# Hybrid layers on one core: a four-tile top-k search with sums on TensorE, weight halves kept in DRAM for the scans, and the product with D moved behind the second group's scan

## The reference

```python
# state space layer: a scan over 512 tokens, 1024 channels, 16 states each
dA = jnp.exp(dt_t[..., None] * A)
state = state * dA + (dt_t * u_t)[..., None] * B_t[:, None, :]
y = jnp.einsum('bdn,bn->bd', state, C_t)
...
y = ys + x * D
y = y * silu(gate)

# top-k feed-forward: of 1376 values per row the 688 smallest in size become 0
s = silu(x @ w_gate.T)
_, idx = top_k(-abs(s), 688)
s = s.at[rows, idx].set(0) * (x @ w_up.T)
out = s @ w_down.T
```

## Time and profile before

| | us |
|---|---|
| median of 3 runs | 2920.8 (2917.94 to 2924.18) |
| the profiled execution | 2916.4, span 2914.6 |
| mean granted TensorE clock | 0.904 of full speed |
| first scan stage, about | 612 to 962 |
| second scan stage, about | 1098 to 1453 |
| search with its thresholds | 2560 to 2791 |

### The profile page before, as it was taken

How to read it: one execution, slowest core, us unless ns; L and a number is a source line. 1 busy time by engine, 2 the same in 40 slices (tenths; PEclk the granted TensorE clock), 3 DMA queues, 4 the chain that set the end, 5 groups by cost and what they waited for, 6 DMA issues and landing times.

```text
span 2914.6 us, 36546 instructions
## 1 busy us (share of the span) xinstructions
PE 2389.8 (82%) x12216; PEld 1868.3 (64%) x12216; DVE 2028.0 (70%) x3132; ACT 1596.3 (55%) x3341; POOL 1147.3 (39%) x986
## 2 busy tenths in 40 slices
PE   6986889858888866888889799998799998975058
PEld 4334337657777655777777578886678886764046
DVE  3642743659989657989853577875677875489896
ACT  1451551257787227887620276665176665499952
POOL 3022026343243514233357547674547674531100
PEclk9698799969999978999999899999999999985579
DMA  6214122120110111021023201121201121210000
GB/s 214 45 54 147 35 62 80 40 76 23 48 37 23 55 55 39 13 62 30 26 62 99 71 26 55 48 62 44 58 26 55 48 62 44 70 47 21 4 1 29
DMA packets 86257, 152.83 MB, mean 52 GB/s; under 512 B 8664, under 2 KB 17496, under 8 KB 85944
## 3 DMA queue, kind: packets, MB, share of 16 engines
q1 hardware_dynamic: 86072, 150.50, 18.1%
HBM read 135.33 MB, written 14.75 MB: 51 GB/s over the span
## 4 chain that ended last, share of the span: by engine, by line
PE 48%; DVE 18%; ACT 14%; issue 8%; POOL 1%; DVEq 0%; ACTq 0%; POOLq 0%
PE ps L659 42%; PE ps L673 5%; ACT tables L1402 5%; DVE m L1638 2%; DVE m L1664 2%; DVE f_lo L1464 2%; ACT m L1266 1%; DVE m_front L1585 1%; PE ps L798 1%; DVE loose L1567 1%; DVE f_hi L1463 1%; ACT L1266 1%; ACT m L1245 1%; DVE stat L1479 1%; ACT tables L1235 1%
## 5 line engine op out<-in xcount | busy, mean ns | idle before, releaser
L599 POOL TENSOR_SCALAR w_hi<-w_in 128x512 fp32r<-128x512 f32 x408 | 331.8, 813 | 1176.8 <-PE ps L659 614.7
L600 POOL TENSOR_TENSOR w_lo<-w_in,w_hi 128x512 fp32r<-128x512 f32 x408 | 607.6, 1489 | 34.0
L659 PE MATMUL ps<-hT_hi,w_lo 128*128 128x512 f32 x864 | 364.7, 422 | 28.5 <-DVE a L1509 12.3
L659 PE MATMUL ps<-hT_lo,w_hi 128*128 128x512 f32 x864 | 347.2, 402 | 0.0
L659 PE MATMUL ps<-hT_hi,w_hi 128*128 128x512 f32 x864 | 347.0, 402 | 0.0
L1664 DVE TENSOR_TENSOR_SCAN m<-m,m 128x1028 f32<-128x1028 f32 x128 | 315.9, 2468 | 10.3 <-ACT m L1266 3.1
L659 PEld LDWEIGHTS ps<-m,tables 128*128 128x128 f32 x2048 | 258.0, 199 | 53.6 <-ACT tables L1235 25.5
L659 PE MATMUL ps<-m,tables 128*128 128x128 f32 x2048 | 263.2, 284 | 33.0 <-ACT tables L1235 32.8
L673 PE MATMUL ps<-tables,m 128*128 128x128 f32 x1024 | 145.2, 285 | 99.4 <-DVE m L1664 71.4
L1235 ACT ACTIVATE tables<-ps 128x512 f32<-128x512 f32 x256 | 139.1, 593 | 147.2 <-PE ps L673 147.1
L1266 ACT ACTIVATE m<-m_rows,negA 128x256 f32<-128x256 f32 x512 | 217.8, 504 | 0.4
(11 more groups left out here) (256 smaller groups left out, 5269.1 us busy)
## 6 DMA issues: line engine op xcount, KB each, us to landing
w_in<-units SPq DMA_DIRECT2D x419, 256.0 KB, 2.6
stack_scratch<-a SPq DMA_DIRECT2D x48, 256.0 KB
a<-stack_scratch SPq DMA_DIRECT2D x64, 192.0 KB, 4.4
m<-bc_scratch SPq DMA_DIRECT2D x16, 512.0 KB, 5.4
out<-x_sb SPq DMA_DIRECT2D x2, 1024.0 KB, 4.3
tables<-small SPq DMA_DIRECT2D x1, 1143.0 KB, 10.3
x_sb<-x SPq DMA_DIRECT2D x4, 256.0 KB, 3.4
x_sb<-x SPq DMA_DIRECT2D x1, 1024.0 KB, 7.9
```

The lines of the kernel that those rows point to most:

```text
L599: c["did"](nc.gpsimd.tensor_scalar(w_hi[:, r], raw, 1.0, 1.0, ALU.mult, ALU.mult), s["unit_hi"])
L600: c["did"](nc.gpsimd.tensor_tensor(w_lo[:, r], raw, w_hi[:, r].bitcast(F32), ALU.subtract), s["unit_split"])
L659: ins = T.matmul(out, lhsT, rhs, start=start, stop=stop)
```

## The change

1. **Search.** `K_DVE` goes from [1, 2] to [2, 2], so DVE and ACT take 4 tiles each. DVE's compare now writes +0.5 or -0.5 as bf16 and accumulates nothing. PE sums these: 8 chunks of 172 columns per tile, multiplied by a bf16 identity and accumulated in one bank per batch. DVE reduces the 2 x 172 sums, and one update covers all four tiles of a batch. The up-projection uses 6 banks and is cut into half blocks that stand between the sums in PE's queue.
2. **Weight halves.** The 31 units that the scans use are written back to DRAM as two halves when the first feed-forward splits them. In the scans SP loads both halves directly into `w_hi` and `w_lo`; POOL does nothing for them.
3. **`skip` and held outputs.** `skip` moves behind the recurrence of g == 1. PE's sums for group 0 of a tile (`outputs(0, .)`) move behind the transposes of group 1.

```diff
-K_DVE = [1, 2]
+K_DVE = [2, 2]
+K_CHUNK = INTER // 8
+K_BANKS = 6
...
+            def load_halves(u):
+                slot, n = u % RING, halves[u]
+                if n == 0:
+                    for r in range(2):
+                        sp.wait_ge(half_out[r], 32 * len(range(r, len(wanted), 2)))
+                if n >= 4:
+                    sp.wait_ge(half_in[n % 4], 32 * (n // 4))
+                sp.wait_ge(s["unit_used"], u - RING + 1)
+                for part, dst in enumerate((w_hi, w_lo)):
+                    sp.dma_start(dst[:, slot].bitcast(F32), halves_d[halves_at[order[u]], part]).then_inc(half_in[n % 4], 16)
...
+                if n >= RING_IN and stored[ready]:
+                    k = stores[ready]
+                    if k >= 2:
+                        sp.wait_ge(half_out[k % 2], 32 * (k // 2))
+                    for part, src in enumerate((w_hi, w_lo)):
+                        sp.dma_start(halves_d[halves_at[order[ready]], part], src[:, ready % RING].bitcast(F32)).then_inc(half_out[k % 2], 16)
...
+                    if direct[u]:
+                        continue
...
+                        if stored[u - RING]:
+                            k = stores[u - RING]
+                            pool.wait_ge(half_out[k % 2], 32 * (k // 2 + 1))
...
+                        if k == RING:
+                            pool.wait_ge(s["k_thr"], B)
...
                 states_turned(0)
                 states_turned(1)
+                if g == 1:
+                    outputs(0, 0)
+                    outputs(0, 1)
                 piece = ff_beside(local)
                 if piece:
                     ff_piece(1 - b, *piece)
-                outputs(g, 0)
-                outputs(g, 1)
+                if g:
+                    outputs(g, 0)
+                    outputs(g, 1)
...
+                def sums(b, n):
+                    o = claim(K_BANKS + b, summed[b])
+                    for t in range(K_DVE[b]):
+                        pe.wait_ge(less[b], K_DVE[b] * n + t + 1)
+                        for r in range(INTER // K_CHUNK):
+                            ins = T.matmul(o[:, t * K_CHUNK:(t + 1) * K_CHUNK], k_ident, k_low[b][t][:, r * K_CHUNK:(r + 1) * K_CHUNK],
+                                           start=r == 0, stop=(r + 1) * K_CHUNK == INTER)
+                    ins.then_inc(total[b], 1)
+
+                for n in range(K_BITS):
                     for b in range(B):
...
+                        sums(b, n)
+                        if n < B * TT * len(TK_W):
+                            up(n, b)
...
                 dve.wait_ge(s["m_u"], n + 1)
-                if held and g == 1:
-                    skip()
...
                     .then_inc(s["m_h"], 1)
+                if held and g == 1:
+                    skip()
...
-                        V.tensor_scalar(k_junk[:, (n + b + t) % 2], k_abs[b][t], k_cand[:, b].bitcast(F32)[:, t:t + 1], None, ALU.is_lt, ALU.add,
-                                        accum_out=k_cnt[:, b, t:t + 1]).then_inc(less[b], 1)
+                        V.tensor_scalar(k_low[b][t], k_abs[b][t], k_cand[:, b].bitcast(F32)[:, t:t + 1], 0.5, ALU.is_lt, ALU.subtract)\
+                            .then_inc(less[b], 1)
...
-                    dve.wait_ge(less[b], m * (n + 1))
-                    go(V.tensor_scalar(k_no[:, b, 0:m], k_cnt[:, b, 0:m], TOPK - 0.5, bit, ALU.is_ge, ALU.mult))
+                    dve.wait_ge(total[b], n + 1)
+                    did(V.tensor_reduce(k_diff[:, b, 0:m], ps[:, K_BANKS + b, 0:m * K_CHUNK].rearrange("p (t c) -> p t c", t=m), AX.X, ALU.add), summed[b])
                     dve.wait_ge(count[b], (TT - m) * (n + 1))
-                    did(V.tensor_scalar(k_no[:, b, m:], k_diff[:, b, m:], 2.0 * TOPK - INTER - 0.5, bit, ALU.is_ge, ALU.mult))
+                    did(V.tensor_scalar(k_no[:, b], k_diff[:, b], -0.5, bit, ALU.is_ge, ALU.mult))
```

More of the change, by code:

```diff
@@ L257, in hybrid_layers @@
     order = [u for it in items for u in item_units(it)]
+    direct = [it[0] == "scan" for it in items for _ in item_units(it)]
+    wanted = sorted({order[u] for u in range(len(order)) if direct[u]})
+    halves_at = {name: k for k, name in enumerate(wanted)}
+    stored = [order[u] in halves_at and order[u] not in order[:u] for u in range(len(order))]
+    raw = [sum(not d for d in direct[:u]) for u in range(len(order) + 1)]
+    raw_units = [u for u in range(len(order)) if not direct[u]]
+    stores = [sum(stored[:u]) for u in range(len(order) + 1)]
+    halves = [sum(direct[:u]) for u in range(len(order) + 1)]
     down_units = [u for u, name in enumerate(order) if name[0] in ("fd", "mo", "td")]
@@ L274, in hybrid_layers @@
         max_in = [s["a_max_in_0"], s["a_max_in_1"]]
-        cand, less, count = ([s[f"k_{n}_{b}"] for b in range(B)] for n in ("cand", "less", "count"))
+        cand, less, count, total, summed = ([s[f"k_{n}_{b}"] for b in range(B)] for n in ("cand", "less", "count", "sum", "summed"))
         stack_out = [s["a_stack_out_0"], s["a_stack_out_1"]]
@@ L423, in hybrid_layers @@
         stack_d = nc.dram_tensor("stack_scratch", (B, 2, A_HEADS, 3, A_DK, L), F32, kind="Internal").ap()
+        halves_d = nc.dram_tensor("halves_scratch", (len(wanted), 2, P, 512), F32, kind="Internal").ap()
         bc_d = nc.dram_tensor("bc_scratch", (B, N_ST, L), F32, kind="Internal").ap()
@@ L1069, in topk, with up @@
             def topk(_):
-                for j, w in enumerate(TK_W):
+                def up(n, part):
+                    j, b, t = n // (B * TT), n // TT % B, n % TT
+                    o = claim(n % K_BANKS, s["k_up_kept"]) if part == 0 else ps[:, n % K_BANKS]
+                    w, rows_w = TK_W[j], slice(t * P, (t + 1) * P)
+                    for k in range(2 * part, 2 * part + 2):
+                        hi, lo = unit(("tu", j, k), k)
+                        mm3(o[:, 0:w], hT_hi[:, b, k, rows_w], hT_lo[:, b, k, rows_w], hi[:, 0:w], lo[:, 0:w],
+                            k == 0, k == HC - 1, s["k_up"] if k == HC - 1 else None)
+                    if part and n % (B * TT) == B * TT - 1:
+                        release(HC)
+                def sums(b, n):
[7 more added lines that the diff above has]
+                for n in range(K_BITS):
                     for b in range(B):
-                        for t in range(TT):
-                            rows(claim(b * TT + t, s["k_up_kept"]), [("tu", j, k) for k in range(HC)], hT_hi[:, b], hT_lo[:, b], t, w, s["k_up"], b)
-                    release(HC)
+                        sums(b, n)
+                        if n < B * TT * len(TK_W):
+                            up(n, b)
                 def turn_tile(q):
@@ L1879, in threshold @@
                     late, thr = c_b[:, m:], c_b.bitcast(F32)
-                    k_low, k_high, k_up = (k_late[:, n, 0:TT - m] for n in range(3))
+                    k_lower, k_high, k_up = (k_late[:, n, 0:TT - m] for n in range(3))
                     dve.wait_ge(cand[b], K_BITS + 1)
-                    for r in range(B):
-                        dve.wait_ge(less[r], K_DVE[r] * K_BITS)
                     for t in range(m, TT):
@@ L1926, in topk @@
                     V.memset(k_cand[:, b], 1 << K_BITS - 1).then_inc(cand[b], 1)
-                before = counted(lambda b: range(K_DVE[b]))
+                assert 2 * TOPK == INTER
+                did(V.tensor_copy(k_ident, ident))
                 for n in range(K_BITS):
```

68 lines of the change are left out of this document (43 added, 25 removed).

## The result

Over 4 runs the changed kernel takes 2884.15 us (2875.25 to 2894.0), the kernel before on the same chip 2919.37. The ratio is 0.9886 with a 95% interval of 0.9838 to 0.9933: 20 to 47 us faster. The forecast was 2828 us, its range 2775 to 2880.

What follows compares the result with a forecast made beforehand. No engine was full; DVE was busiest in the scans, ACT set the search's pace. Scans -75, search -17, thresholds -1 made -93 from 2916.4, or 2823.4; with 4.4 for the median, 2828 us, range 2775 to 2880.

Steps and rivals of the forecast that it cites:

- Search, thresholds: Search stage and the thresholds after it: search falls to 204 us, 17 us less, and thresholds give 1 us more.
- (b): Search: DVE's compare runs at one element a cycle, adding 67 us to the forecast, 2895 us in all; chance 0.11.
- (d): Search: PE's sums bound it and the kernel gets slower, 207 us above forecast, 3035 us; chance 0.04.
- the 6 us for late sums: Search: allowance of 6 us for updates that find their sum from PE late.
- POOL's stretch of DVE: Scans: POOL no longer splits 58 units of weights, at 1.02 us each, so DVE is busy 59 us less.
- Rival (c): Scans: DMA writes, not POOL, stretch DVE, so 59 us less 10 are not gained, 2877 us; chance 0.03.
- skip: Scans: moving skip behind the second group's recurrence saves 36 of the 44.4 us DVE waits for PE's sums.
- The held outputs: Scans, g == 1: the same 8 products cost PE nothing but make it late by up to 2 us.
- DVE stays the bound by a few per cent only: Scans: DVE's 64 x 4.3 = 275 us against PE's 259 plus time-step matmuls and a cold start.
- the 20 us given back: Scans: 20 us of the gain come back as new waits, 10 a scan.
- the 60 of my bound: Scans: upper bound of 60 us on the gain that returns as new waits; the lower is 0.
- Rival (a): Scans: PE and ACT take over, DVE's savings become waits, 60 us returned instead of 20, 2868 us; chance 0.17.

Runs made afterwards that it cites:

- sh: Search change and stored weight halves on the kernel before, with skip and the first outputs in their old places: median 2871.5 us, scan stages 781.3 us.
- shk_ts: Full change with PE's time-step products moved to g == 1 and ACT's first time-step rows behind the kept states: median 2866.9 us, scan stages 771.0 us.
- skip_ts: Full change with the first outputs not held and the time-step products moved to g == 1: median 2873.7 us, scan stages 779.6 us.

## Why the prediction was wrong, step by step

- **Search, thresholds:** right (-20.8 against -18 with the tail), and so were its parts: compare 936 ns, reduction 508. The compare is stretched to at most 2056 ns while POOL splits; over 124 compares the mean is 1028, so the stretch is 124 x 0.092 = 11.4 us, the 12 that I had put down. Rivals (b) and (d) are out. Against the 6 us for late sums stand 18.8 us of ACT's waits for updates, of which the stretch is a part.
- **POOL's stretch of DVE:** right, 54.5 us against 59. Rival (c) is out: DMA's share rose from 0.15 to 0.22 and the recurrence's median is 2.30 us.
- **skip:** the waits in front of it fell by 32.4 us (44.4 to 4.4 + 7.6), against 36. But as a gain that was worth next to nothing: on top of the halves the moved `skip` gives 2.0 us of the stages.
- **"The held outputs ... cost nothing on PE but make it late by up to 2 us there":** wrong. They cost 12.4 us with `skip` moved and 41 with `skip` in place. In the latter case PE has nothing to fill the gap while DVE waits for the last sums. The waits fit that reading (between the first and the last recurrence of the first scan, PE's for recurrences are 34.0 us against 22.9 in `sh`, DVE's in front of `skip` 37.2 against 28.1), but no run isolates it. I had looked at what PE's queue holds, and not at who waits for what is delayed in it.
- **"DVE stays the bound by a few per cent only", and the 20 us given back:** this is the step that failed. From the forecast's own terms, -54.5 of stretch and -32.4 of waits should have given -86.9; the stages gave -19.1, so 68 us came back in place of 20, above the 60 of my bound. Of these 12.4 are the hold's; the other 55 came back without it. I set DVE's 4.3 us a group against PE's 4.04, as if the scan were the longer of two sums. In the code it is a ring: three slots of states and of decays, and each group goes DVE, PE, ACT, PE; that this ring sets the length is argued, and no run changed the number of these slots. ACT, whose busy sum is the smallest, was left out of the comparison, while the windows show that the length isn't any engine's sum, and a cut of 45 us there gives 24 a stage. Before the change a cut of either DVE or ACT gave 37 us over both stages; after it DVE's cut gives 6.4.
- **Rival (a)**, PE and ACT take the scans over, came nearest: 68 us came back rather than 60, with ACT in front rather than PE, and with the hold, which it does not name, in the sum. Its 2868 lies 16 us below the result: 8 are the waits above its 60, 8 the stretch and `skip` terms (-95 against -86.9), less 3 for the search; the last 3 are inside the measurement. That measurement was coarser than the 6 us that I gave it: the interval of the ratio is 14 us to either side.

**The version to keep.** `shk_ts` has the shortest scans with nothing left out and the ring of loads at four (771.0), and the lowest median (2866.9; `sh` 2871.5). Both beat the kernel before by about 2% (ratios 0.9798 and 0.9801) and the change by some 14 us (0.9849). The difference of their medians is inside the spread; by the scan stages `shk_ts` is 10 us better.

**Left open.** Where the hold costs with `skip` in place, outside the groups with time steps, was not isolated; nor why ACT's microseconds count most, which fits its being needed twice in each group (decays and copies) with table loads between, but no run tells that from other readings.

## What to carry to other kernels

Where three engines pass each group around a ring, a busy sum does not name the bound, and waits on the least busy engine are not slack: 68 us off DVE gave 3 us here, 45 us off ACT gave 24. Price a microsecond on each engine, at the place where it would be taken, before trading work, and before holding work back in a queue list what stands behind it. A wait's name is not its cause until the resource has been doubled and the time has gone with it. When whole-kernel times scatter by 10 us through the clock of an untouched stage, measure the touched stage between fixed marks.

## What the runs showed of the hardware

- A VectorE compare of 1376 float32 to bf16 without an accumulated sum takes 936 ns; the accumulating one took 1645. Beside POOL it goes up to 2056 ns, which the accumulating one never did (1649 at most).
- The Trainium skill's page "GPSIMD Engine Reference", section "Key points", says that the two contend where VectorE runs in a 2-port mode. The trace agrees in that this compare is stretched, 11.4 us in all against 17 by that rule with the scans' price; in which mode it ran no run shows.
- The attention stage, 194 us at a granted clock of 0.91, took 226 us at 0.71 in `skip_ts` with the same instructions.
